# Statistics of the second norm from accumulated sums, four residual passes closer together, and another order in the opening and the first slot

## What is computed

```python
x = x + xattn(layernorm(x), ctx, ctx)      # 16 heads of 32, 154 context rows, causal mask
x = x + ffn(layernorm(x))                  # eps 1e-5 in both norms

def xattn(q, k, v):
    q, k, v = q @ Wq.T + bq, k @ Wk.T + bk, v @ Wv.T + bv
    a = softmax(mask(q . k / sqrt(512)))
    return (a . v) @ Wo.T + bo

def ffn(x):
    h = bit_linear(x, w1)                  # 512 -> 2048
    h = silu(depthwise_conv1d(h, conv_w, conv_b))   # 3 taps over the rows
    return bit_linear(h, w2)               # 2048 -> 512

def act_quant(x):                          # per row
    scale = 127 / clip(max|x|, 1e-5)
    return clip(round(x * scale), -128, 127) / scale
def bit_linear(x, w):                      # w is rounded to -1, 0, 1, scaled by mean|w|
    return act_quant(x) @ weight_quant(w).T
```

## Time and profile before

| | |
|---|---|
| median of three timed runs | 1595.4 us (1593.45 to 1602.17) |
| the profiled execution, its own time | 1609.67 us |
| its span | 1607.9 us, 24773 instructions |
| PE busy | 92% of the span |
| DVE, ACT, POOL busy | 84%, 71%, 64% |
| mean granted PE clock | 0.953 of full speed |
| DMA | 85.21 MB, mean 53 GB/s |

### The profile page before, as it was taken

How to read it: one execution, slowest core, us unless ns; L and a number is a source line. 1 busy time by engine, 2 the same in 40 slices (tenths; PEclk the granted TensorE clock), 3 DMA queues, 4 the chain that set the end, 5 groups by cost and what they waited for, 6 DMA issues and landing times.

```text
span 1607.9 us, 24773 instructions
## 1 busy us (share of the span) xinstructions
PE 1486.2 (92%) x9097; PEld 906.9 (56%) x9097; DVE 1353.2 (84%) x2078; ACT 1146.0 (71%) x2028; POOL 1032.0 (64%) x838
## 2 busy tenths in 40 slices
PE   9799797999999999999999999999999999998776
PEld 6377364746565564747465665647474656655322
DVE  7565788798988989898889889897979898878896
ACT  3445596968688795959587787959586877878552
POOL 4101186768587685858586876858575867868462
PEclk8967799999999999999999999999999999999987
DMA  8540201012130303021220303031310302020000
GB/s 258 138 137 33 67 8 41 27 36 69 27 93 7 93 8 93 8 53 47 52 66 7 93 8 93 8 86 23 67 41 9 91 8 67 8 67 1 30 27 27
DMA packets 80343, 85.21 MB, mean 53 GB/s; under 512 B 29983, under 2 KB 55839, under 8 KB 79709
## 3 DMA queue, kind: packets, MB, share of 16 engines
q1 hardware_dynamic: 80221, 83.62, 19.2%
HBM read 38.74 MB, written 19.42 MB: 36 GB/s over the span
## 4 chain that ended last, share of the span: by engine, by line
PE 40%; DVE 36%; ACT 18%; issue 4%; POOL 3%; DMA 0%; DVEq 0%; ACTq 0%; SPq 0%
PE ps L861 12%; DVE negm L1738 10%; PE ps L867 8%; PE ps L1043 5%; ACT h L1268 4%; DVE r L1659 4%; DVE pm L1659 4%; ACT hqb L1165 3%; ACT h L1263 3%; ACT pexp L1244 3%; PE ps L830 3%; DVE h L1650 3%; DVE xn L1713 2%; DVE xr L1720 2%; PE ps L679 2%
## 5 line engine op out<-in xcount | busy, mean ns | idle before, releaser
L654 POOL TENSOR_TENSOR h<-h,r 128x512 f32<-128x512 f32 x240 | 306.9, 1327 | 102.4 <-ACT r L1165 102.4
L644 POOL TENSOR_TENSOR h<-h,gall 128x512 f32<-128x512 f32 x235 | 344.1, 1464 | 18.4
L642 POOL TENSOR_TENSOR gall<-gall,cw 128x512 f32<-128x512 f32 x235 | 257.5, 1096 | 118.8 <-DVE h L1650 118.8
L1650 DVE SCALAR_TENSOR_TENSOR h<-gall,cw,h 128x512 f32<-128x512 f32 x256 | 265.6, 1040 | 58.2 <-ACT h L1263 58.0
L861 PEld LDWEIGHTS ps<-va,pexp 128*128 128x128 f32 x2048 | 269.7, 198 | 30.1 <-issue 13.1
L861 PE MATMUL ps<-va,pexp 128*128 128x33 f32 x2048 | 267.3, 276 | 0.0
L867 PE MATMUL ps<-xqT,w1T 128*128 128x512 f16 x1024 | 257.7, 382 | 7.7 <-DVE gall L1575 7.4
L1575 DVE SCALAR_TENSOR_TENSOR gall<-ps,bias,srow 128x512 f32<-128x512 f32 x256 | 191.1, 747 | 79.0 <-POOL h L644 48.0
L1043 PE MATMUL ps<-w2T,hqb 128*128 128x512 fp8e4 x960 | 249.8, 390 | 0.0
L1244 ACT ACTIVATE pexp<-ps 128x512 f32<-128x512 f32 x320 | 179.7, 588 | 70.2 <-PE ps L830 27.9
L1263 ACT ACTIVATE h<-gall,cb,cw 128x512 f32<-128x512 f32 x256 | 221.9, 867 | 8.5
(11 more groups left out here) (220 smaller groups left out, 2328.2 us busy)
## 6 DMA issues: line engine op xcount, KB each, us to landing
qs<-hl SPq DMA_DIRECT2D x192, 128.0 KB, 2.6
xr<-in_x SPq DMA_DIRECT2D x16, 1024.0 KB, 5.5
out<-xr SPq DMA_DIRECT2D x64, 256.0 KB
h<-in_L_ffn_w SPq DMA_DIRECT2D x8, 1024.0 KB, 5.5
srow<-in_L_xattn_bo SPq DMA_DIRECT2D x15, 256.0 KB, 3.2
kst<-kh_scratch SPq DMA_DIRECT2D x32, 38.5 KB
xr<-in_ctx SPq DMA_DIRECT2D x1, 1024.0 KB
h<-in_L_xattn_Wk SPq DMA_DIRECT2D x1, 1024.0 KB, 8.4
```

What stands on the lines that cost most here:

```text
L642: gp.tensor_tensor(right, right, cw[:, c, 2:3].to_broadcast([P, TB]), ALU.mult).then_inc(c2m_ok, 1)
L644: gp.tensor_tensor(hc(c), hc(c), right, ALU.add).then_inc(c2p_ok, 1)
L654: gp.tensor_tensor(hc(c), hc(c), r2[:], ALU.mult).then_inc(u_ok, 1)
L1650: ve.scalar_tensor_tensor(out=hc(c), in0=g[:, c % 4, 1:TB + 1], scalar=cw[:, c, 1:2], in1=hc(c), op0=ALU.mult, op1=ALU.add).then_inc(c1_ok, 1)
```

## The change

- **Residuals.** `residual(i)` is one instruction: the pass also writes the sum of the new row (`accum_out`, one column of `sum2`). bn_stats and bn_aggr of the second norm go (8 instructions on DVE per slot, 16 slots).
- **Centring.** ACT's `centre(i)` writes sum - 512 x, 512 times the centred row with the sign turned, which it can do from the sum alone. There are now four buffers for it (all of `xn`) in place of two. `centre(2)` waits for the end of the output projection, which reads that memory too; the wait on `centred_max` is gone.
- **Variance.** New on ACT: `square(i)`, four per slot, the square of the centred row with its sum accumulated in a column of `sq2`. `norm2` is now sums / 512 + eps and waits for the four squares. Two multiplications in `quantise` take the factor 1/512 along, in the same instructions.
- **Order on DVE, regular slots.** Three residuals, `centred_max(0)`, the fourth residual; `norm2` goes from behind the fourth residual to between the second and third `q_low`, and `quantise` behind the fourth.
- **Order on ACT.** `centre` 0 to 3 with the two first `offset` between, then four squares, then `offset(2)`.
- **Slot -1.** DVE does the four `w_abssum` first, then the four `q_low`.
- **Slot 0.** DVE does the four `q_low` ahead of the residuals, and the first eight `maximum` ahead of `quantise`; ACT's four `w2_half` stand behind its rounding passes.

The lists of PE, POOL and SP are as before. The diff, cut to its core:

```diff
         nb1 = sb("nb1", [P, TT], F32)
-        st2 = sb("st2", [P, TT, 6], F32)
-        mv2 = sb("mv2", [P, TT, 2], F32)
+        sum2 = sb("sum2", [P, TT], F32)
+        sq2 = sb("sq2", [P, TT], F32)
         nw2 = sb("nw2", [P, 4, TT], F32)
...
-            return xn[:, 2 + i % 2, :]
+            return xn[:, (i + 2) % 4, :]
...
         x2_ok = sem("x2_ok")
-        bn_ok = sem("bn_ok")
-        ag_ok = sem("ag_ok")
+        sv_ok = sem("sv_ok")
         zx_ok = sem("zx_ok")
...
                 def centre(i):
-                    act.wait_ge(ag_ok, at(s, TT, i + 1))
-                    if i >= 2:
-                        act.wait_ge(za_ok, at(s, TT, i - 1))
-                    nc.scalar.activation(centred(i), ring(s)[:, i, :], ACT.Identity, bias=mv2[:, i, 0:1], scale=-1.0).then_inc(zx_ok, 1)
+                    act.wait_ge(x2_ok, at(s, TT, i + 1))
+                    if i == 2:
+                        act.wait_ge(op_ok, at(s, TT, TT))
+                    nc.scalar.activation(centred(i), ring(s)[:, i, :], ACT.Identity, bias=sum2[:, i:i + 1],
+                                         scale=-float(D)).then_inc(zx_ok, 1)
+
+                def square(i):
+                    act.wait_ge(zx_ok, at(s, TT, i + 1))
+                    nc.scalar.activation(osb[:, i, :], centred(i), ACT.Square, scale=1.0 / D,
+                                         accum_out=sq2[:, i:i + 1]).then_inc(sv_ok, 1)
...
                         w_round(0, i)
-                for i in range(TT):
-                    if s == 0:
-                        w2_half(i)
-                    if do_a:
-                        centre(i)
-                    if late_results(s) and i != 2:
-                        offset((0, 1, 2, 2)[i])
+                if do_a:
+                    centre(0)
+                    if late_results(s):
+                        offset(0)
+                    centre(1)
+                    centre(2)
+                    centre(3)
+                    if late_results(s):
+                        offset(1)
+                    for i in range(TT):
+                        square(i)
+                    if late_results(s):
+                        offset(2)
                 if s == 1:
...
                                              scale=qm1[:, 3, i:i + 1]).then_inc(xq_ok, 1)
+                if s == 0:
+                    for i in range(KT):
+                        w2_half(i)
                 if late_results(s):
...
                     ve.scalar_tensor_tensor(out=ring(s)[:, i, :], in0=OB[i], scalar=1.0 / WS, in1=ring(s)[:, i, :],
-                                            op0=ALU.mult, op1=ALU.add).then_inc(x2_ok, 1)
-                    dve.wait_ge(x2_ok, at(s, TT, i + 1))
-                    ve.bn_stats(st2[:, i, :], ring(s)[:, i, :]).then_inc(bn_ok, 1)
-                    dve.wait_ge(bn_ok, at(s, TT, i + 1))
-                    ve.bn_aggr(mv2[:, i, :], st2[:, i, :]).then_inc(ag_ok, 1)
+                                            op0=ALU.mult, op1=ALU.add, accum_out=sum2[:, i:i + 1]).then_inc(x2_ok, 1)
...
                 def norm2():
-                    dve.wait_ge(ag_ok, at(s, TT, TT))
-                    ve.tensor_scalar(nw2[:, 0, :], mv2[:, :, 1], EPS, None, ALU.add).then_inc(ln2, 1)
+                    dve.wait_ge(sv_ok, at(s, TT, TT))
+                    ve.tensor_scalar(nw2[:, 0, :], sq2[:], 1.0 / D, EPS, ALU.mult, ALU.add).then_inc(ln2, 1)
...
                     dve.wait_ge(za_ok, at(s, TT, TT))
-                    ve.tensor_tensor(qm1[:, 0, :], qx[:], nw2[:, 2, :], ALU.mult).then_inc(ln2, 1)
+                    ve.scalar_tensor_tensor(out=qm1[:, 0, :], in0=qx[:], scalar=1.0 / D, in1=nw2[:, 2, :],
+                                            op0=ALU.mult, op1=ALU.mult).then_inc(ln2, 1)
                     dve.wait_ge(ln2, at(s, 10, 5))
...
                     dve.wait_ge(ln2, at(s, 10, 8))
-                    ve.scalar_tensor_tensor(out=qb[:, 0, :], in0=mv2[:, :, 0], scalar=-1.0, in1=qm1[:, 3, :],
+                    ve.scalar_tensor_tensor(out=qb[:, 0, :], in0=sum2[:], scalar=-1.0 / D, in1=qm1[:, 3, :],
                                             op0=ALU.mult, op1=ALU.mult).then_inc(ln2, 1)
...
                     merge()
+                if s == 0:
+                    for k in range(NG):
+                        q_low(k)
                 if do_a:
...
                     residual(1)
+                    residual(2)
                     centred_max(0)
-                    residual(2)
+                    residual(3)
                     centred_max(1)
-                    residual(3)
-                    norm2()
                 if do_f:
...
                     centred_max(3)
+                if s > 0 and do_q:
+                    q_low(0)
+                    q_low(1)
+                if do_a:
+                    norm2()
+                if s > 0 and do_q:
+                    q_low(2)
+                    q_low(3)
+                if s == 0:
+                    for n in range(8):
+                        maximum(n // NG, n % NG)
+                if do_a:
                     quantise()
-                if do_q:
+                if s == -1:
                     for k in range(NG):
-                        if s == -1:
-                            w_abssum(0, k)
+                        w_abssum(0, k)
+                    for k in range(NG):
                         q_low(k)
-                if s == -1:
                     w_scales(0)
...
                         scaled(c)
-                for n in range(TT * NG):
+                for n in range(8 if s == 0 else 0, TT * NG):
                     if do_q:
```

## The result

The changed kernel takes 1547.64 us (median of four runs, 1545.25 to 1549.65) against 1598.18 us before (four runs, 1593.45 to 1602.17): ratio 0.9684, 95% interval 0.9648 to 0.9721, some 50 us or 3.2% faster. The forecast was 1562.0 us, its range 1550 to 1584. The profiled execution took 1545.68 us with a span of 1543.9 us. Of the 49 later executions of the kernel before, two took 2538 and 3732 us; why is open, and no figure here counts them.

A forecast was written before the change was run, and what follows sets the result against it. TensorE, busy 92%, was taken as the bound, its main recurring wait turn_pm for VectorE's residuals (30.1 us). Terms 24.2 + 10.1 + 7.3 - 5.0 + 1.8 = 38.4 us, 33.4 with clock halved, took 1595.4 to 1562.0 us; range 1550 to 1584.

The forecast's parts named there:

- Residuals in a row: Slots 2 to 14: with residuals 0.75 us each, turn_pm's wait falls to 0.1 us per slot, winning 24.2 us.
- The size of the gap itself: At turn_pm, slot 5: PE starts 2.12 us after the output projection's last matmul ends, waiting for the third residual.
- The query scores: Regular slots: VectorE meets PE with 0.2 us to spare; the 0.38 us wait is left as is, counted as nothing.
- Clock: Behind the gap, six slots lose 1.69 us each at half clock; 10.1 us won in all, half of it counted.
- the drops do not belong to the gap: Rival, regular slots: clock drops stay or timed runs never had them; 28.3 us won, 1567; inside the 0.66 forecast case.
- Opening: Slot -1: sums of |w1| ahead of q_low remove PE's 6.76 us wait; 7.3 us won with the first query scores.
- Slot 0: End of slot 0: norm2 waits for squares, the row maxima copy stands behind four w2_half; 5.0 us lost.
- Slot 0 keeps its clock: Rival, slot 0: shorter idle time ahead keeps the clock up, some 15 us more won, 1547; chance 0.08.
- Slots 1 and 15: Slot 1 wins 0, its gain lost waiting for w2_copy; slot 15 wins 1.8 us from the earlier third residual.
- Dear reads: Rival, regular slots: 0.86 us per residual and 1.0 per square leave waits at gap and maxima; about 1578; chance 0.13.
- no change: Rival, regular slots: the gap moves to the query scores, only opening and slot 0 count; 1593; chance 0.08.
- slower: Rival, every slot: squares of 1.7 us on ScalarE delay norm2 and PE, 1610; chance 0.05.

The follow-up runs named there:

- regular_only: Changed kernel with slot -1 and slot 0 both put back as before, leaving the change in slots 1 to 15: 1557.6 us, ratio to before 0.9735.
- order_only: Kernel before with three residuals in a row in every slot, bn_stats and bn_aggr staying on VectorE: 1587.7 us, ratio to before 0.9936.
- open_only: Kernel before with only slot -1 edited, the four sums of |w1| first, then the four q_low: 1591.2 us, ratio to before 0.9966.
- gap_longer: Changed kernel with four unread bn_stats passes between second and third residual from slot 1 on: 1589.4 us, ratio to before 0.9944.
- slot0_back: Changed kernel with only slot 0's order put back as before: 1546.2 us, ratio to before 0.9665.
- both_ahead: Changed kernel with slot 0's four w2_half right behind the squares and three row maxima ahead of norm2: 1541.2 us, ratio to before 0.9653.
- both_again: Same kernel as both_ahead, run once more with more executions: 1540.7 us, ratio to before 0.9644.
- after_again: The changed kernel, unedited, run again beside other runs: 1550.8 us, ratio to before 0.9694.

## Why the prediction was wrong, point by point

- **What bounds the kernel, and where the change acts:** right. The `turn_pm` waits are gone, the regular slot is shorter, and regular_only has 42 of the 50 us.
- **Residuals in a row:** right in kind, under-sized by 5.3 us (26.0 against 31.3): the wait that I left in (1.3 us), slot 15 (1.0, by its idle entry), and the overlap of the next point (2.2) are most of it. I took 0.75 us for a residual with its sum. They start 0.61 us apart, and in order_only, where nothing is accumulated, three take 1.88 us, 0.60 apart. The Trainium skill (VectorE: DVE Perf Modes, "Two Vector instructions with no wait between them") counts such an op as two instructions, and the trace agrees that there are two: the row DVE_READ_ACCUMULATOR, 0.08 us. But it runs while the next pass starts, and the path sees 0.01 us of it. My "gain is excluded, 0.67 at least" priced a hidden row as a visible one, with an overlap of 0.09 us already read four lines above it.
- **The size of the gap itself:** I took the 2.12 us of the earlier trace rows for the wait. It is counted from the modelled end of the matmul ahead (609.20), but without the wait `turn_pm` starts 0.16 us before that end. So each idle entry hides 0.16 us more: 2.28 us per slot, and 2.2 us over fourteen.
- **The query scores:** this step failed. "I leave the 0.38 us where it is": it went, with its own hidden overlap 0.70 us in slot 5, 5.0 us in all, in a term that my sum put at nothing. My sum gave DVE 0.2 us to spare there; it has 0.70. The cause is the same, 0.8 us for a square where it is 0.61, 0.75 for a residual where it is 0.61: counted from the first residual, DVE was to be free for the maxima after 12.8 us and is after 11.9.
- **Clock:** the term was right, 10.1 against 9.8 us, and then I halved it, on the guess that the profiled execution's excess over the median (14.3 us) meant fewer drops in the timed runs. open_only has the drops in the same six slots, in another execution, and gap_longer in five of them. The excess lay in slot 0 by the profiles: 37.5 us in a row at 1.2 GHz there, against 10.2 us in open_only's at 1596.67 us. That guess cost 4.7 us. The rival that the drops do not belong to the gap fell with gap_longer. What was said for it, seven slots with the same gap and no drop, was misread: of slots 2, 4, 5, 8, 9, 12 and 13 only 5, 9 and 13 have it (2.09 to 2.12 us by the idle entry), slots 4, 8 and 12 have 1.8 and slot 2 has 0.7.
- **Opening:** 7.3 us forecast, 6.8 in the pairing, 5.4 and 6.6 in the two kernels that have it alone or lack it alone.
- **Slot 0:** the mechanism was right in each step: `norm2` waits 1.45 us for the squares, PE 4.39 us for the maxima and 5.34 us for the copy behind four `w2_half`. With 20.8 us, the lead ahead of this stretch, added to the times after, the first maximum is at 170.7 us (171.7 forecast), the rounding passes end at 182.1 (182.6), the copy is at 189.1 (190.2) and the first score of slot 1 at 195.0 (195.8). So -3.8 us, not -5.0, and slot0_back gives -3.0; the first microsecond is the square again, 0.61 and not 0.8.
- **Slot 0 keeps its clock**, the rival at 1547: the profiles show it, 14.0 us between these two executions, and its number, 1547, is nearly the measured one. That is luck: without these 14.0 us the profiles differ by 50.0, which is what the medians show, and both kernels have executions of either kind. That the two kernels have them equally often is not shown.
- **Slots 1 and 15:** 0 and 1.8 us forecast. In slot 1 the 1.96 us at `turn_pm` came, and only some 0.8 us went back at `w2_copy` and behind it. In slot 15 it was 2.9 us.
- **Dear reads, no change, slower:** none came. The first two would have shown as brackets at `turn_pm` and at the query scores, and there are none in slots 2 to 14.

From the 33.4 us that were forecast: 5.3 more at the gap, 5.0 at the scores, 4.7 of clock that was not to be halved, 2.0 in slot 1, 1.2 in slot 0 and 1.2 behind slot 15, less 2.3 of small losses (the table's last row but one) and 0.5 in the opening: 50.0 us, against 50.5 measured. Apart from the clock and slot 1, the large ones come from taking the dear side where a hidden overlap stood in the rows.

## What to carry to other kernels

Taking a wait away pays only if what stands behind it is earlier too: here the order alone gave 10 to 13 us, and with the statistics out of that engine's list, which brought its first row maximum some 3 us forward, the regular slots gave 42. Here an idle entry behind pipelined matmuls understated the wait by the 0.16 us of overlap that the next one would have had, and passes that followed each other cost their distance (0.61 us), not their duration (0.68); over fourteen slots that decides the sum. When the profiled execution stands off the median, look for the stretch that differs between executions of one kernel before discounting any term.

## What the runs showed of the hardware

- An accumulated sum is a row of its own, 0.08 us on VectorE (64 rows, 5.3 us) and 0.19 us on ScalarE (64 rows, 11.9 us). Passes with one start 0.61 us apart on both engines. On VectorE that is 0.01 us more than without; on ScalarE no run has squares without a sum beside them.
- Gaps of 2.25 to 2.76 us ahead of 32 matmuls brought 3.4 us at 1.2 GHz in five or six slots of nine, those of 1.73, 1.95 and (in one slot) 2.15 us in none; the slots were nearly the same in three kernels (3, 6, 7, 10, 11, 14). Why those, no run shows. In one execution of both_ahead 13.7 us at 1.2 GHz came behind three waits of 0.47 to 0.75 us.
- For the same program the clock in the first 140 us is not the same from one execution to the next (at most 10 us in a row at 1.2 GHz from 85 us on in both_again, 51 us in both_ahead). It put 14.6 us between these two profiles by slot 1, and the six executions of after_again lie 17 us apart, a third of what this change is worth.
